# Reading a block's four offset words at its opening, ahead of the wait for the scaled sums

## The reference, cut to what matters

```
msg  = h[src, edge_type]                                   # 206,250 edges
seg  = dst * R + edge_type                                 # R = 8
sums = segment_sum(msg, seg, num_segments=n * R)
cnt  = segment_sum(ones,  seg, num_segments=n * R)
mean = sums / maximum(cnt, 1.0)[:, None]
agg  = mean.reshape(n, R, -1).sum(axis=1)
h    = relu(agg + x @ root + bias)                         # twice; then a linear by node type
```

## Time and profile before

| what | value |
|---|---|
| time, median of 3 runs | 4575.01 us (4574.68 to 4577.68) |
| span of the profiled execution | 4574.0 us, 121525 instructions |
| TensorE matmuls busy | 3738.4 us, 82% |
| TensorE weight loads busy | 3272.6 us, 72% |
| VectorE busy | 3166.8 us, 69% |
| GpSimd busy | 3246.8 us, 71% |
| ScalarE busy | 892.6 us, 20% |

### The profile page before, as it was taken

One profiled execution on the slowest core, in us unless ns is written; L12 is line 12 of the kernel. 1 busy time (PEld: TensorE's weight loads), 2 busy tenths in 40 slices (PEclk: granted clock), 3 DMA queues, 4 the chain that ended last, 5 costly groups with the idle time before them and its releaser, 6 DMA issues.

```text
span 4574.0 us, 121525 instructions
## 1 busy us (share of the span) xinstructions
PE 3738.4 (82%) x38021; PEld 3272.6 (72%) x38022; DVE 3166.8 (69%) x8385; ACT 892.6 (20%) x2493; POOL 3246.8 (71%) x3382
## 2 busy tenths in 40 slices
PE   2476677777767767767549999999999999999999
PEld 2355555555555555555438999999999999999998
DVE  6577677777777777776646767676676767677674
ACT  5000000000000000000003333333333333333333
POOL 1677777777777777777567777777777777777770
PEclk6565665665656656655559999999999999999999
DMA  6666655565555555555466666565656566656661
GB/s 211 181 194 195 174 168 168 165 168 168 165 168 168 164 168 166 167 168 164 122 170 173 173 173 169 170 171 168 169 168 172 167 172 174 170 170 168 171 171 21
DMA packets 359003, 762.96 MB, mean 167 GB/s; under 512 B 130103, under 2 KB 182108, under 8 KB 358657
## 3 DMA queue, kind: packets, MB, share of 16 engines
q0 software_dynamic: 215360, 663.86, 51.3%
q1 hardware_dynamic: 129381, 81.62, 6.6%
q10 hardware_dynamic: 14112, 16.06, 1.0%
HBM read 725.50 MB, written 35.78 MB: 166 GB/s over the span
## 4 chain that ended last, share of the span: by engine, by line
PE 57%; DVE 20%; issue 12%; POOL 6%; DMA 3%; ACT 1%; DVEq 0%; POOLq 0%; SPq 0%; ACTq 0%
PE bank L1469 15%; PE bank L1482 15%; PE bank L1382 12%; DVE mixed L1015 7%; DVE inv L1048 6%; POOL slot L593 5%; PE bank L1414 4%; PE bank L1378 4%; PE bank L1444 3%; PE bank L1445 2%; DVE scaled L1055 2%; DVE hot L1030 2%; DMA slot<-table,idx 2%; DVE inv L1047 1%; DVE mixed L1013 1%
## 5 line engine op out<-in xcount | busy, mean ns | idle before, releaser
L593 POOL DMA_INDIRECT slot<-table,idx x3354 | 3234.9, 965 | 1191.5 <-issue 979.4
L1382 PE MATMUL bank<-hot,slot 128*128 (+1 forms) x21168 | 1252.5, 213 | 62.7 <-DMA slot<-table,idx 54.1
L1382 PEld LDWEIGHTS bank<-hot,slot 128*128 128x128 bf16 x21168 | 1002.3, 108 | 125.2 <-issue 68.6
L1378 PE MATMUL bank<-hot,ones_b 128*128 x1764 | 401.3, 227 | 650.0 <-DVE scaled L1055 225.1
L1378 PEld LDWEIGHTS bank<-hot,ones_b 128*128 128x128 bf16 x1764 | 181.4, 103 | 936.0 <-issue 877.9
L1469 PE MATMUL bank<-root_sb,ffn_w 128*128 128x128 f32 x6272 | 772.9, 278 | 0.0
L1482 PE MATMUL bank<-ffn_w,act 128*128 128x256 f32 x3136 | 756.7, 384 | 1.0 <-DVE root_sb L1142 0.7
L1469 PEld LDWEIGHTS bank<-root_sb,ffn_w 128*128 128x128 f32 x6272 | 741.4, 192 | 8.0
L1482 PEld LDWEIGHTS bank<-ffn_w,act 128*128 128x128 f32 x3136 | 569.5, 190 | 64.9 <-issue 1.1
L1015 DVE SCALAR_TENSOR_TENSOR mixed<-scaled,small,mixed 128x256 f32<-128x256 f32 x1372 | 573.7, 481 | 12.2
L1015 DVE SCALAR_TENSOR_TENSOR mixed<-scaled,comp_sb,mixed 128x256 f32<-128x256 f32 x1372 | 573.4, 480 | 10.5
(11 more groups left out here) (158 smaller groups left out, 2407.5 us busy)
## 6 DMA issues: line engine op xcount, KB each, us to landing
slot<-table,idx POOLq DMA_INDIRECT x3354, 3.1
inv<-inv_d SPq DMA_DIRECT2D x98, 256.0 KB
table<-ffn_w SPq DMA_DIRECT2D x7, 1344.0 KB, 5.5
table<-parts ACTq DMA_DIRECT2D x49, 192.0 KB, 2.9
ffn_w<-in_L_ffn_W_dram SPq DMA_DIRECT2D x16, 512.0 KB, 5.3
typed_x_d<-zn ACTq DMA_DIRECT2D x49, 128.0 KB, 3.2
zn<-in_x_dram SPq DMA_DIRECT2D x48, 128.0 KB
root_sb<-typed_x_d SPq DMA_DIRECT2D x48, 128.0 KB
```

Source lines behind the costliest of these rows:

```text
L593: gp.indirect_dma_start(out=slot[:, k, :], out_offset=None, in_=table[layer], in_offset=bass.IndirectOffsetOnAxis(ap=idx[:, h, k:k + 1], a ...
L1378: t.matmul(C[:, at], ones_b[:, :], oh, start=(k == 0), stop=(k == TILES - 1), skip_group_check=True)
L1382: last = t.matmul(S[f][:, at], slot[:, k, q * D + f * P:q * D + (f + 1) * P], oh, start=(k == 0 and q == 0), stop=(k == TILES - 1 and q == ...
```

## The change

Opening a block now waits for the one-hots first, adds one to a new semaphore `pe_waited` (an instruction that the wait rides on), reads all four words of offsets into four registers of the block, and only then waits for the scaled sums. The tiles use the registers and read nothing. The reads stay four per block, 784 in all.

```
@@ Block.__init__ @@
                     self.at = slice(b, b + 1) if static else bass.ds(b, 1)
+                    pe.wait_ge(hot_ready, n + 1)
+                    pe.sem_inc(pe_waited, 1)
+                    self.words = []
+                    for w in range(WORDS):
+                        self.words.append(pe.alloc_register(f"word{next(loads)}"))
+                        pe.reg_load(self.words[w], off[0:1, self.one, w:w + 1])
                     pe.wait_ge(sc_ready, n + START)
-                    pe.wait_ge(hot_ready, n + 1)
                     self.full = 16 * n + 16 if static else pe.snap(n * 16 + 16, min_val=16)
@@ Block.tile @@
                     else:
-                        if field == 0:
-                            self.word = pe.alloc_register(f"word{next(loads)}")
-                            w = (k - 1) // FIELDS
-                            pe.reg_load(self.word, off[0:1, self.one, w:w + 1])
-                        col = bass.RuntimeValue.of_register_unchecked(self.word, min_val=0, max_val=1 << 27)
+                        col = bass.RuntimeValue.of_register_unchecked(self.words[(k - 1) // FIELDS], min_val=0, max_val=1 << 27)
                         col = (col >> (FIELD * field)) & (SLOTS - R)
```

More of the change, by code:

```diff
@@ L249, in build @@
         sp_waited = sem("sp_waited")
+        pe_waited = sem("pe_waited")
         s_dve = sem("s_dve")
```

## The result

The changed kernel takes 4606.76 us (median of 4 runs, 4605.75 to 4607.76) against 4575.61 (median of 4) for the kernel before. The ratio is 1.0066, with a 95% interval of 1.0055 to 1.0078: slower by 31 us, which is small and clear of the noise. The profiled execution has a span of 4605.2 us against 4574.0.

A forecast was written before the change was run, and what follows sets the result against it. Gathers were taken to bound the first layer, TensorE the second. First layer 0, stalls at h = 0 36.8 us, less 6.6 us back, make 30 us: 4605 us on the median. Likeliest case 4590 to 4625; 8 in 10, 4583 to 4640.

The forecast's parts named there:

- The place: Second layer: the h = 0 opening stalls, its cover being 1.03 us; the h = 1 opening costs 0.
- The price of a read in a row: TensorE's sequencer, block openings: 0.36 us per read, four reads 1.44 us; bounds 0.10 and 0.46 us.
- The rival in which reads overlap: Reads in a row at 0.10 us each, h = 0 stall under 0.1 us, time 4571 us; chance 0.13.
- the one in which they are slower in a row: Reads 0.6 us or more each, or sequencer not catching up: 4697 us, or 4640 at half; chance 0.07.
- The stall: Second layer, h = 0: TensorE stands still 0.8 us before `ups(5)`, 46 times, 36.8 us.
- The gain: Second layer, fifth group of h = 1: 0.52 us instead of 0.66 without its read, 47 x 0.14 = 6.6 us back.
- The first layer: 0 us: gathers pace it, and the opening reads lie under DVE's scaling with 0.5 us to spare.
- TensorE's 29% of idle time is spare: First layer: TensorE is busy 71%, gathers set the pace, so the remaining 29% is spare.
- Rival 2: If TensorE, not POOL, paced the first layer, 186 us would go, 4390 us; chance 0.04 including a small form.
- The rule that the sequencer pushes an engine instruction and goes on: At h = 0, reads would begin under ACT's work, from about 3016.3: no stall, 4568 us; the prediction rejected it.

The follow-up runs named there:

- run 2: Changed kernel, but in the second layer only the h = 1 opening reads the four words together; h = 0 reads each at its first tile: 4571.4 us.
- run 3: Changed kernel, but in the second layer only the h = 0 opening reads the words together; h = 1 reads each at first use: 4612.27 us.
- Run 4: Changed kernel, but h = 0 waits for its one-hots and reads its words ahead of the logits; the scaled sums' wait stays: 4574.59 us.
- run 10: Changed kernel, but each opening in the second layer's loop reads eight words in a row, four from another small table: 4728.22 us.
- Run 1: Changed kernel, but words are read together in the first layer only; the second reads each at its first tile: 4575.24 us.
- run 8: Kernel before, but from the second pair on two of three first-layer gathers fetch 16 rows instead of 128: 4554.57 us, ratio 0.9954.
- run 9: Changed kernel with reads together in the first layer only, plus lighter gathers (two of three fetch 16 rows): 4490.04 us, ratio to before 0.9811.
- run 5: Changed kernel, but the second layer's h = 0 opening reads only two words together, the others at tiles 9 and 13: 4573.16 us.
- run 7: Changed kernel, but the second layer reads words at first use and its h = 0 opening has fourteen more semaphore adds: 4644.2 us.

## Why the prediction was right

**The place.** It said that only the h = 0 opening of the second layer has too little work in hand. Runs 2 and 3 divide the change by place: without the reads at h = 0 the loss is gone, with these alone it is all there. Run 4 shows the reason too: begun ahead of the wait for ScalarE, the same four reads cost 0.07 us.

**The price of a read in a row.** 0.36 us was the working value, with 0.10 and 0.46 as bounds. Measured: 0.37 (four in the changed kernel, eight in run 10). In the first layer, where a register instruction goes with each read, they stand 0.47 us apart, and the prediction had 0.46. The four reads of one opening of the first layer, changed kernel:

```profile
L1357 PEldq TENSOR_LOAD <-off x4: 297/304/309, 1023.8 to 1025.2; - x4
```

The rival in which reads overlap is refuted, and so is the one in which they are slower in a row; the longest in the second layer of the changed kernel takes 0.33 us.

**The stall.** Predicted 0.80 us, measured 0.74 on average over 46 turns, and 0.82 in run 3. That 0.80 came so close is in part luck, for two small terms of the prediction were wrong in opposite ways: from `sem_inc` to the first read pass 0.15 us and not 0.10, and from line 1468's instruction to the first matmul of `ups(5)` 0.11 us and not 0.20. The difference between 0.74 and 0.82 is a step that the prediction didn't have: a wait for ScalarE's gelu ahead of `downs(3)`. The kernel before had 0.16 us to spare there (gelu ends at 3014.94 + 1.14 = 3016.08; `downs(3)` begins at 3016.24). Timeline of ScalarE, kernel before, then timelines of ScalarE and TensorE, changed kernel, one turn later than the one above:

```profile
3014.94 1.14 ACT L770 ACTIVATE act<-bank,small 128x128 f32<-128x128 f32 x4
```

```profile
3069.54 1.14 ACT L771 ACTIVATE act<-bank,small 128x128 f32<-128x128 f32 x4
...
3070.73 1.99 PE L1484 MATMUL bank<-ffn_w,act 128*128 128x256 f32 x8
```

In the changed kernel gelu ends at 3070.68, `downs(3)` begins 0.05 us later and lasts 1.99 us instead of 1.89. TensorE comes 0.15 us earlier out of the fifth group and so arrives before ScalarE; on average 0.08 us go.

**The gain.** Predicted 0.14 us a turn, measured 0.15 at its place (0.13 in the fifth group, 0.02 in the two records behind it), but 0.07 net of that wait. Per turn: 0.74 - 0.15 + 0.08 = 0.67, against 0.664 measured; predicted 0.80 - 0.14 = 0.66. The sum came out closer than its terms, because the wait that was overlooked takes from the gain what it gives to the stall. 46 x 0.664 = 30.5 us of the 31.2 between the two spans; the remaining 0.7 us is of the size by which the second layer's begin differs (0.6).

**The first layer.** Predicted 0, since the gathers pace it and the reads fit ahead of the wait for the sums. Run 1 shows 0 (ratio 1.0001), the waits of TensorE show where the gain went, and runs 8 and 9 show that it is a gain that is hidden and not one that is absent: 67 us appear when GpSimd's pace per gather is made shorter by 4%. One reading was too generous, that TensorE's 29% of idle time is spare: in run 8, with nothing changed on TensorE, the first layer gets only 1.1% shorter before GpSimd has to wait for TensorE. Most of the idle time of the kernel before consists of waits for the scaled sums (191.4 us from 400 to 2200 us), the sequencer (181.2) and the gathers (130.3). In run 8 the waits for gathers are gone, but the first two stay (214.7 and 189.6 us). The forecast of 0 didn't rest on the size of the spare time, for the change could only add to it. Rival 2 had the mechanism of that gain right, and its condition (real waits in POOL's idle time) is what run 8 created.

**The sequencer and a waiting weight load.** The rule that the sequencer pushes an engine instruction and goes on (the Trainium skill, "Perfetto Trace Analysis", Sequencer Loop) would have let the reads begin under ScalarE's work. The trace does not agree: in all 46 turns of the changed kernel line 1352 starts 0.06 us behind ScalarE's end, as line 1351 does in the 46 of the kernel before, and run 4 gains all but 0.07 us of the stall by placing the reads ahead of the waiting load. Run 4 does not show how many instructions the sequencer may push behind one that waits; that stays open.

No version that computes the right sums is clearly faster than the kernel before. Runs 2 and 5 have turns of 44.49 us, 0.06 shorter than before, which makes 3 us; their intervals (0.9984 to 1.0004 and 0.9986 to 1.0005) include no change.

## What to carry to other kernels

In this kernel, instructions that TensorE's sequencer carries out itself cost nothing while the engine has queued work, and their full length beyond it (four reads of 1.5 us in all, 0.7 to 0.8 us of stall; fourteen semaphore adds of 2.1 us, 1.5 us). Before moving them, look for the last wait that holds the sequencer and count the work that is queued behind it; put them ahead of that wait. Reads that are spread out each fit under a little cover, and a row of four needs all of it in one place. And before counting a gain on one engine, look whether the one that paces the stretch ever waited for it.

## What the runs showed that I had not expected

- Semaphore adds in a row come 0.15 us apart (run 7), register instructions 0.10, though both are recorded with 0.04 to 0.05 us.
- Most of a gather's price on GpSimd doesn't depend on its rows: in run 8 (1000 to 1600 us), where two of three fetch 16 rows, the shortest takes 0.835 us and the median 0.873; with 128 rows throughout the shortest takes 0.942 and the median 0.949.
- The long reads of the first layer, up to 0.78 us, are gone when the reads stand at the opening. Line 1357, changed kernel, the first layer and the four reads of the second layer's first opening:

```profile
L1357 PEldq TENSOR_LOAD <-off x396: 296/299/327, 129.8 to 2301.2; - x198
```

  What stretched them inside a block was not tried.
